# A four-part graph network: the softmax passes in 30 groups, of 3, 4, 26 times 7, 4 and 3 tiles, and some operations of ScalarE and VectorE in another order

## What is computed

```python
h = relu(layernorm(x)); x = x + L0(h)     # two graph attention layers (GAT), self loops added
h = relu(layernorm(x)); x = x + L1(h)     # graph transformer: exp(clip(k[src] . q[dst]))
h = relu(layernorm(x)); x = x + L2(h)     # attention with one head, then tanh(|u|) * u / |u|
h = relu(layernorm(x)); x = x + L3(h)     # two GCN layers and a projection

def gat_layer(x, src, dst, W, a_src, a_dst, b):        # 4 heads of 64
    feat = x @ W
    e = leaky_relu(al_s[src] + al_d[dst], 0.2)
    m = segment_max(e, dst)
    ee = exp(e - m[dst]); s = segment_sum(ee, dst)
    return segment_sum(ee / (s[dst] + 1e-16) * feat[src], dst) + b
# L0: gat_layer, elu, gat_layer
# L2: scores = h[src] @ a_s + h[tgt] @ a_t; softmax by target as above
#     u = h + segment_sum(h[src] * weight, tgt); tanh(|u|) * u / |u|, norm clipped at 0.95
```

## Time and profile before

| | us |
|---|---|
| median of 3 runs | 5120.69 (5118.16 to 5121.72) |
| the profiled execution, its own time | 5117.03 |
| its span, first to last instruction | 5115.2 |
| pass 1, about | 1469 to 2233 |
| pass 2, about | 2233 to 2886 |
| L1's pass, about | 2886 to 3700 |
| pass 3, about | 3700 to 4186 |

### The profile page before, as it was taken

One profiled execution on the slowest core, in us unless ns is written; L12 is line 12 of the kernel. 1 busy time (PEld: TensorE's weight loads), 2 busy tenths in 40 slices (PEclk: granted clock), 3 DMA queues, 4 the chain that ended last, 5 costly groups with the idle time before them and its releaser, 6 DMA issues. The chain is left out here.

```text
span 5115.2 us, 74853 instructions
## 1 busy us (share of the span) xinstructions
PE 4351.1 (85%) x20185; PEld 3272.2 (64%) x20185; DVE 4034.4 (79%) x13139; ACT 2974.8 (58%) x7633; POOL 3123.2 (61%) x2813
## 2 busy tenths in 40 slices
PE   3999999999958888857888799999867749988887
PEld 2888888888836666645666466666544427765555
DVE  5899999999968788759999388888767769955554
ACT  2999999999934444424555377777645534521111
POOL 3766666666446666537777665555554436647777
PEclk9999999999978999978999899999977769999898
DMA  4888888888854444338898456656468866644443
GB/s 136 296 311 312 309 311 308 310 309 310 302 178 125 133 135 134 117 94 282 300 301 283 154 179 188 189 184 184 146 213 268 267 197 201 208 140 136 148 157 127
DMA packets 652112, 1097.58 MB, mean 215 GB/s; under 512 B 85506, under 2 KB 472458, under 8 KB 651573
## 3 DMA queue, kind: packets, MB, share of 16 engines
q1 hardware_dynamic: 532418, 838.42, 48.0%
q0 software_dynamic: 119168, 253.97, 16.7%
q10 hardware_dynamic: 112, 0.40, 0.0%
HBM read 524.78 MB, written 575.95 MB: 215 GB/s over the span
## 5 line engine op out<-in xcount | busy, mean ns | idle before, releaser
L855 PE MATMUL mm<-w,tt 128*128 128x264 f32 x3136 | 732.5, 387 | 2.6 <-ACT tt L899 2.6
L1424 POOL DMA_INDIRECT got<-F,index x392 | 529.7, 1351 | 264.0 <-PE acc L1607 158.9
L855 PEld LDWEIGHTS mm<-w,tt 128*128 128x128 f32 x3136 | 582.3, 191 | 93.0 <-ACT tt L899 2.8
L1603 PE MATMUL acc<-got,sel 128*128 128x260 f32 (+1 forms) x1176 | 437.7, 460 | 108.3 <-DVE sel L1578 100.1
L1616 ACT ACTIVATE rows<-acc 128x260 f32<-128x260 f32 (+1 forms) x588 | 226.8, 386 | 497.3 <-PE acc L1607 497.1
L821 POOL DMA_INDIRECT place<-PLACE,place_ix x392 | 413.2, 1054 | 119.5 <-issue 119.5
L2761 DVE SCALAR_TENSOR_TENSOR agg<-mask,agg,acc 128x128 f32<-128x128 f32 x784 | 247.8, 344 | 254.9 <-PE acc L2748 140.9
L793 POOL DMA_INDIRECT xd<-in_x_dram,index x196 | 224.9, 1148 | 316.8 <-DMA XD<-xd 285.0
L855 PE MATMUL mm<-wl,tt 128*128 128x264 f32 x1568 | 413.1, 386 | 0.6 <-ACT tt L899 0.6
L1607 PE MATMUL acc<-rows,carry 128*128 128x260 f32 (+1 forms) x1008 | 358.0, 440 | 47.5 <-ACT rows L1616 44.1
L1294 PE MATMUL kv<-wkv,ht 128*128 128x512 f32 x784 | 372.7, 598 | 0.1
(11 more groups left out here) (414 smaller groups left out, 12951.8 us busy)
## 6 DMA issues: line engine op xcount, KB each, us to landing
F<-f1o SPq DMA_DIRECT2D x97, 528.0 KB
F<-f2o SPq DMA_DIRECT2D x97, 528.0 KB
HL<-ho SPq DMA_DIRECT2D x97, 528.0 KB
xin<-in_x_dram SPq DMA_DIRECT2D x97, 512.0 KB, 5.7
H<-h SPq DMA_DIRECT2D x97, 512.0 KB, 3.2
X<-x3o SPq DMA_DIRECT2D x97, 512.0 KB, 3.3
out_dram<-oo SPq DMA_DIRECT2D x97, 512.0 KB
drow<-DSTF SPq DMA_DIRECT2D x84, 448.0 KB
```

The source lines that it names most:

```text
L855: last = nc.tensor.matmul(mm[PAIR[stage, q]][:, r, 0:F2W], lhs[:, q, 2 * r + k, :], w[:, k, :], start=(k == 0), stop=(k == KB - 1))
L1424: nc.gpsimd.indirect_dma_start(out=buf[:, n % SLOTS, t, :], out_offset=None, in_=table, in_offset=bass.IndirectOffsetOnAxis(ap=index[:, n ...
L1603: nc.tensor.matmul(acc, self.sel[:, s, t, :], self.got[:, n % SLOTS, t, 0:w], start=True, stop=False)
```

## The change

1. The 196 tiles are cut into 30 groups, of 3, 4, 26 times 7, 4 and 3 tiles, in all three softmax passes. Every operation on a group has its group's own width. Buffers keep their size. The tables that say which tiles belong together (`across_tiles`, `whole`, `beyond`) get their entries for the four short groups by operations of their own in the preamble of pass 1. The degree gathers beside pass 2, on the pool queue, are 118 within the loop and 39 behind it, for 112 and 42.
2. Pass 1, ScalarE: Relu and Exp of group x stood together in slot 6. Relu now stands in slot 4 behind the exponents, Exp in slot 5.
3. Pass 2: nothing but the sizes.
4. Pass 3, VectorE: the part for x (den, reciprocal, hc) stands ahead of the part for c (var, rsqrt, unc). ScalarE: tanh stands behind the copy of row 5, where it stood behind the copy of row 3.

```diff
-PIECES = (slice(0, 4), slice(4, 7))
...
-    NS = T // GS
+    SIZES = (3, 4) + (GS,) * (T // GS - 2) + (4, 3)
+    NS = len(SIZES)
...
+    def tiles_before(n):
+        return sum(SIZES[0:max(n, 0)])
+
+    def size(n):
+        return SIZES[n] if 0 <= n < NS else GS
+
+    def tiles_of(n):
+        return slice(tiles_before(n), tiles_before(n + 1))
+
+    def pieces(n):
+        return (slice(0, 4), slice(4, size(n))) if size(n) > 4 else (slice(0, size(n)),)
...
-                for t in range(GS):
+                for t in range(size(n)):
+                    tile = tiles_before(n) + t
                     nc.gpsimd.indirect_dma_start(
...
+                for n in range(NS):
+                    if size(n) < GS:
+                        link.go(V.memset(across_tiles[:, n, :, :], -BIG))
+                        last = tiles_before(n + 1) - 1
+                        link.go(V.memset(whole[:, 1, last:last + 1], 0.0))
+                        link(V.memset(beyond[:, 1, last:last + 1], -BIG))
...
+                    for n in range(NS):
+                        if SIZES[n] < GS:
+                            first = slots.start
+                            V.tensor_scalar(table[:, n, k, :, first:first + size(n)],
+                                            whole[:, k, tiles_of(n)].unsqueeze(1).to_broadcast([P, HQ, size(n)]),
+                                            -1.0, BIG, ALU.add, ALU.mult)
...
                             if within(a) and t == 4:
                                 ph.exponents(act, a)
-                            if within(x) and t == 6:
+                            if within(x) and t == 4:
                                 hold(act, d["x"], x + 1, None)
                                 hold(act, d["g"], x, None)
-                                nc.scalar.activation(zm[:, :, :], o[:, x % SLOTS, :, :], ACT.Relu, scale=-1.0)\
+                                nc.scalar.activation(zm[:, 0:size(x), :], o[:, x % SLOTS, 0:size(x), :], ACT.Relu, scale=-1.0)\
                                     .then_inc(d["neg"], 1)
+                            if within(x) and t == 5:
                                 hold(act, d["neg"], x + 1, None)
-                                nc.scalar.activation(zm[:, :, :], zm[:, :, :], ACT.Exp, scale=-1.0)\
+                                nc.scalar.activation(zm[:, 0:size(x), :], zm[:, 0:size(x), :], ACT.Exp, scale=-1.0)\
                                     .then_inc(d["exp"], 1)
...
-                            if within(c) and t == 3:
+                            if within(c) and t == 5:
                                 hold(act, d["unc"], c + 1, None)
-                                nc.scalar.activation(th[:, :], unc[:, :], ACT.Tanh).then_inc(d["tanh"], 1)
+                                nc.scalar.activation(th[:, 0:size(c)], unc[:, 0:size(c)], ACT.Tanh).then_inc(d["tanh"], 1)
```

More of the change, by code:

```diff
@@ L1308, in edge_rows, with group_rows @@
             return table[bass.ds(n * (tiles * P) + first, tiles * P), :].rearrange("(t p) w -> p t w", p=P)
-        late = [t for t in range(T) if t % GS >= IN_SECOND]
+        def group_rows(table, n):
+            first = table.shape[0] - EP + tiles_before(n) * P
+            return table[first:first + size(n) * P, :].rearrange("(t p) w -> p t w", p=P)
+        early = [range(T)[tiles_of(n)][0:IN_SECOND] for n in range(NS)]
+        late = [t for n in range(NS) for t in range(T)[tiles_of(n)][IN_SECOND:]]
         def gather_degrees(pool, tiles, bound):
@@ L1391, in ratio, with turned_top, last_rows @@
             def ratio(self, n):
-                return self.wt[:, n % 2, self.kinds * GS * self.h:(self.kinds * GS + 1) * self.h]
+                first = self.kinds * size(n) * self.h
+                return self.wt[:, n % 2, first:first + self.h]
+            def turned_top(self, n):
+                return self.top[:, 0:self.h * size(n)].rearrange("p (h t) -> p h t", h=self.h)
+            def last_rows(self, n):
+                return self.rows[:, 1 - n % 2, size(n - 1) - 1, :]
             def start_pool(self, pool):
@@ L1454, in gathered @@
                 for group in self.fetched:
-                    hold(eng, group[n % SLOTS], 16 * GS * (n // SLOTS + 1), None)
+                    hold(eng, group[n % SLOTS], 16 * sum(SIZES[n % SLOTS:n + 1:SLOTS]), None)
             def store(self, sp, n, table, rows, sem, count, stored):
                 hold(sp, sem, count, None)
-                sp.dma_start(edge_rows(table, n, GS), rows).then_inc(stored[n % 2], 16)
+                sp.dma_start(group_rows(table, n), rows[:, 0:size(n), :]).then_inc(stored[n % 2], 16)
             def end_stores(self, sp, *stored):
@@ L1611, in take_rows @@
             def take_rows(self, act, n, t):
-                d, tile = self.done, n * GS + t
+                d, tile = self.done, tiles_before(n) + t
                 if t == 0:
@@ L2126, in group @@
                         for t in range(GS + 2):
-                            if within(b) and t < GS:
+                            if within(b) and t < size(b):
                                 ph.accumulate(pe, b, t)
@@ L2601, in group @@
                             rows = ph.rows[:, x % 2, :, :]
[L2602 to L2604 removed]
+                            g = size(x)
+                            link(V.tensor_scalar(den[:, 0:g], rows[:, 0:g, 258], 1e-10, None, ALU.add))
+                            link(V.reciprocal(den[:, 0:g], den[:, 0:g]))
+                            for t in range(g):
                                 last = V.scalar_tensor_tensor(hc[:, x % 2, t, :], rows[:, t, 0:D], den[:, t:t + 1],
```

303 lines of the change are left out of this document (159 added, 144 removed).

## The result

The changed kernel takes 5183.68 us (median of 4 runs, 5178.03 to 5186.39), the kernel before in the same comparison 5119.42. The ratio is 1.0127, with a 95% interval of 1.0114 to 1.0141. So it is slower, as forecast, and by twice as much: +64 us where I gave +31.5. 5183.68 is at the very edge of the range.

A forecast was written before the change was run, and what follows sets the result against it. It took VectorE to bound pass 2, and loops through several engines passes 1 and 3. Terms 9 + 4.5 + 18 = +31.5 on 5117.0 gave 5148.5, as a median 5152 us; range 5098 to 5184.

The forecast's parts named there:

- the two mechanisms: Pass 1: Relu and Exp queue ahead of the last row copy; pass 3: VectorE waits for tanh, delaying its accumulation-opening product.
- Pass 3: New order in the third softmax pass: period 16.3 to 16.4 against 15.63 over 23 periods; +18 us, from -3 to +35.
- the 10.82 to 12.36 behind it: Third softmax pass: us from TensorE's first product to ScalarE's next Exp of the scores, in a short and a long iteration.
- rival 4: More lower clock: third pass at 17.06 every iteration (+33), first pass losing 0.5 an iteration (+12); 5180 us; chance 0.15.
- Pass 1: First softmax pass: ScalarE's queue before the last row copy makes the period 25.3 against 24.97; +9 us, from -3 to +20.
- a stretch of lower clock is mostly absorbed: First softmax pass: TensorE would be done some 2 us before ScalarE, so its slow stretches would mostly not lengthen the period.
- The sizes, set at 0: First softmax pass, 30 groups: start some 5 us late, end some 5 early; 0, at worst 8 either way.
- Pass 2: Second softmax pass, VectorE-bound: short groups cost +6 twice, partly regained in start and end; +4.5 us, from 0 to +12.
- The sum 6.6 lower: Second softmax pass: alternative estimate with fixed cost 2.7 us a group (45 instructions, 58 cycles each) in place of 6.
- Rival 1: TensorE's clock stays up in the third pass: period 14.0, -38 us there, median 5098 us; chance 0.15.

## Why the prediction was right and wrong

- **The direction** and the two mechanisms were right. So was the cause: undoing the orders takes all of the loss away, undoing the sizes none.
- **Pass 3, +33.3 for +18.** The steps up to the first product were right to 0.03 us each. What was mis-sized is the last one, "with the 10.82 to 12.36 behind it the period is 15.5 to 17.1; I take the middle". The runs show 12.34 to 12.36 behind it in each of the last 19 full iterations. The two values that I took the middle of belong to two different pauses: the 10.82 to a first product 2.91 behind the exponents, the 12.36 to one 4.33 behind them. The new one was to come at 4.70, so the second was its row. The trace of before says so more than once: from 3767.61 on, the four iterations whose first product came 3.92 to 4.46 behind the exponents had 12.35 to 12.68 behind it. The same pause with the same slow stretch behind it comes in iteration after iteration, with a period of 17.07, in the changed kernel, in the two others that have tanh at row 5 and no idle products in pass 3, and in the run with idle products in pass 1. Why they settle at just this value no run shows. The long end of the range was rival 4's price for pass 3, and it had 0.15.
- **Pass 1, +25.4 for +9.** The full-clock period was near (25.3, measured 25.5), partly by luck: the iteration that I read was the last full one, whose differences come 21.50 after crow, where the 23 ahead of it have 21.75 to 21.93, and that error was offset by a queue on ScalarE of 4.7 for my 5.0. The sentence that failed is "a stretch of lower clock is mostly absorbed". I compared TensorE's end with ScalarE's end, and there were 2 us between them. But ScalarE's end is counted from the exponents, and those stand behind a put that waits for TensorE in the middle of the iteration. A delay there goes into the exponents, past Relu and Exp, to crow, in full. The run with TensorE kept busy in pass 1 measures it: 11.8. The sizes, set at 0, are 5 the better with the old orders (760.5 for 765.5), no more than profiles differ by, and make no difference with the new ones (790.9 with 30 groups, 790.8 with 28).
- **Pass 2, +2.5 for +4.5.** The pass with the 30 groups took 654.0 to 655.7 in all runs, with 28 groups 650.3 to 654.2. The term was right in sign and within what one run scatters. The sum 6.6 lower that I gave beside it, by the fixed cost per instruction, would have made pass 2 shorter by 2.1, and it did not get shorter.
- **L3, +7.8 for 0.** The code there is the same. With 30 groups L3 took 928.3 to 937.5 in eight profiles, with 28 groups 928.2 to 932.8 in five. The run with idle products in pass 3 has the same L3 and the same sizes as the changed kernel and took 928.3, for 936.8, so most of the 7.8 can be scatter. Whether the 30 groups have a part in it is open.
- **Rival 1** (the clock stays up) had 14.0 for the period and is refuted, but its number was good: where idle products keep the clock up, the period is 13.79. **Rival 4** came nearest, with 5180. The row that I used against it for pass 1, a clock of 0.96 in spite of a pause of 2.84, says how often the clock falls and not what it costs when it does: with the new order the clock is 0.93 there, and each fall costs up to 2 us. The rule of the Trainium skill that I named with it ("TensorE: Matmul & The Clock Gate", the section on depth-cycling), that frequent short idles between groups of matmuls make the clock swing between its two levels, agrees with the trace in both passes: a pair of products lasts 1.20 and then 0.60 in one iteration of pass 3, 1.07 and then 0.60 in one of pass 1.

## What to carry to other kernels

Where a loop runs through TensorE and has a pause in it, the same work behind the pause has more than one price: 9.06 with the clock up, 10.52 behind the shorter pause, 12.35 behind the longer one. Take the price from an iteration whose pause is as long as the new one will be, and not a mean over iterations with different pauses. A slack is worth what it is at the point where the late engine is waited for, so follow a delay from that point through the queue of the engine that waits, and not from end to end. A large operation that is moved "earlier" into a queue is late for whatever stands behind it; put it behind the last operation that the loop needs, or ahead of the one that is waited for.

## What the runs showed of the hardware

Products that do nothing made the kernel faster: 17 in each iteration of pass 3 took 73 us off it (516.6 to 443.2), with the granted clock of a stretch at 0.99 for 0.70 and nothing else changed. And the lower clock can settle into a fixed pattern: 19 periods in a row within 0.02 us at 17.07, and 11 in a row within 0.01 at 13.65 with tanh behind row 4 and 28 groups. The pattern need not be one period long: in the run with the sizes alone, periods of 15.05, 13.73, 16.82, 16.26 and 16.66 follow one another in this order, to within 0.01, three times.
